# Adapter attention moved: scores and softmax into the front, its product into attention's steady part

## The reference

```python
q, k, v = split(h @ w_attn.T)                      # h: modulated layernorm of x
q, k = rope(q), rope(k)
y = softmax(causal(q @ k.T / sqrt(32))) @ v
_, ak, av = split(adapter_wte @ w_attn.T)          # 10 adapter tokens, no rope
s = q @ ak.T / sqrt(1024)                          # per head: 2048 x 10
y = y + gating[0] * softmax(s) @ av
x = x + ga * (y @ w_proj.T)                        # then a mixture of experts
```

## Time and profile before

| | us |
|---|---|
| median of 3 runs | 2719.55 (2714.84 to 2725.62) |
| the profiled execution, its own time | 2727.61 |
| its span, first to last instruction | 2725.7 |
| front | 0 to 679 |
| attention, head | 679 to 851 |
| attention, steady part | 851 to 1966 |
| its end, and the tail | 1966 to 2725.7 |
| busy PE / DVE / POOL / ACT over the span | 91% / 58% / 48% / 39% |

### The profile page before, as it was taken

The page is one execution under the profiler, slowest core; times in us unless marked ns, Lnnn a source line. Parts: engine busy times, 40 slices in busy tenths (PEclk is TensorE's granted clock), DMA queues, the critical chain, the costliest instruction groups (busy, mean ns, idle before and its releaser), DMA issues. The chain is left out here.

```text
span 2725.7 us, 39161 instructions
## 1 busy us (share of the span) xinstructions
PE 2491.5 (91%) x13391; PEld 1630.1 (60%) x13391; DVE 1593.0 (58%) x3130; ACT 1051.3 (39%) x1860; POOL 1313.7 (48%) x824
## 2 busy tenths in 40 slices
PE   6789999999578999999999999998889876999997
PEld 4667676777454444444444444443368765888885
DVE  5544554210256777777777777777236554777665
ACT  3420011111135655555555555555601111444443
POOL 4351442100365766676766676765724452332332
PEclk8899999999589999999999999998989887999998
DMA  7356556311953524252515151513266745888885
GB/s 265 109 155 201 160 165 183 100 39 51 223 202 103 113 55 111 56 115 54 116 49 120 42 131 40 133 34 79 77 203 216 168 113 183 305 299 294 302 287 178
DMA packets 224849, 397.18 MB, mean 146 GB/s; under 512 B 43756, under 2 KB 94380, under 8 KB 224564
## 3 DMA queue, kind: packets, MB, share of 16 engines
q1 hardware_dynamic: 199588, 319.56, 40.9%
q0 software_dynamic: 17152, 50.38, 5.3%
q10 hardware_dynamic: 7952, 25.21, 2.9%
HBM read 299.16 MB, written 103.76 MB: 148 GB/s over the span
## 5 line engine op out<-in xcount | busy, mean ns | idle before, releaser
L1397 POOL TENSOR_TENSOR t_two<-t_prob 128x1024 f32<-128x1024 f32 (+1 forms) x321 | 688.2, 2164 | 181.1 <-ACT t_prob L1207 107.7
L1207 ACT ACTIVATE t_prob<-t_scores_psum 128x512 f32<-128x512 f32 (+3 forms) x1280 | 611.1, 537 | 387.8 <-PE t_scores_psum L999 194.9
L1237 DVE TENSOR_REDUCE t_part<-t_seen_psum 128x1 f32<-128x512 f32 x768 | 480.8, 681 | 165.3 <-PE t_seen_psum L976 161.0
L976 PE MATMUL t_seen_psum<-t_k_stack,t_q_stack 96*128 96x512 f32 (+3 forms) x1283 | 517.1, 412 | 24.2 <-DVE t_part L1237 15.8
L999 PE MATMUL t_scores_psum<-t_q_stack,t_k_stack 97*128 97x512 f32 (+3 forms) x1280 | 506.1, 407 | 5.9 <-ACT t_prob L1207 4.4
L999 PEld LDWEIGHTS t_scores_psum<-t_q_stack,t_k_stack 97*128 97x128 f32 x1280 | 244.0, 191 | 310.0 <-ACT t_prob L1207 172.4
L1243 DVE CUSTOM_DVE_ANT_0 t_seen_psum<-t_seen_psum,t_causal 128x128 f32<-128x128 f32 (+3 forms) x515 | 250.0, 504 | 106.3 <-PE t_seen_psum L976 96.1
L1019 PE MATMUL t_y_acc_psum<-t_prob,t_v 128*32 128x512 f32 (+3 forms) x2560 | 304.9, 549 | 0.0
L976 PEld LDWEIGHTS t_seen_psum<-t_k_stack,t_q_stack 96*128 96x128 f32 x1283 | 253.2, 199 | 67.1 <-DVE t_part L1237 30.7
L1678 PE MATMUL acc_psum<-z_e_hi,z_x_hi 128*128 128x512 f32 x576 | 228.3, 396 | 0.0
L1680 PE MATMUL acc_psum<-z_e_hi,z_x_lo 128*128 128x512 f32 x576 | 225.2, 391 | 0.0
(11 more groups left out here) (240 smaller groups left out, 3804.1 us busy)
## 6 DMA issues: line engine op xcount, KB each, us to landing
z_raw<-in_expert_w SPq DMA_DIRECT2D x80, 512.0 KB, 5.3
z_spare<-in_expert_w SPq DMA_DIRECT2D x72, 512.0 KB
f_w_raw<-in_wmod SPq DMA_DIRECT2D x8, 2048.0 KB, 10.1
t_q_stack<-scratch_q_hi SPq DMA_DIRECT2D x64, 256.0 KB, 5.3
t_k_stack<-scratch_k_hi SPq DMA_DIRECT2D x64, 256.0 KB, 5.2
f_w_raw<-in_w_attn SPq DMA_DIRECT2D x24, 512.0 KB, 6.1
t_inverse<-scratch_inverse SPq DMA_DIRECT2D x132, 64.0 KB
t_y<-scratch_a_y SPq DMA_DIRECT2D x33, 256.0 KB
```

The lines of the kernel that those rows point to most:

```text
L976: nc.tensor.matmul(seen[:, n % BANKS, 0:width], q_stack[par][0:STACK, h, t0:t0 + P], k_stack[par][0:STACK, h, c * CH:c * CH + width], star ...
L1207: nc.scalar.activation(prob[:, step % RING, h, c0:CH], scores[:, score_bank(step, h), c0:CH], ACT.Exp, scale=1.0 / math.sqrt(D)).then_inc( ...
L1237: nc.vector.tensor_reduce(dst, seen[:, n % BANKS], AX.X, ALU.max).then_inc(seen_free, 1)
L1397: nc.gpsimd.tensor_tensor(two[:, pair % 2, heads, c0:CH], a, b, ALU.add).then_inc(two_ready, 1)
```

## The change

The adapter's scores and softmax move into the front's q units. Ask number m (m = 0 to 31, one per q unit) multiplies the rotated `y` of unit 32 + m with the adapter's k, inside the next unit, behind 21 of its 24 matmuls. DVE subtracts the maximum (`lower`), ACT takes the exponential (`exponent`), DVE sums and inverts (`invert`), POOL multiplies (`spread`), SP stores 80 KB of probabilities to `a_prob_d`. POOL's `low_y` of a q unit now also waits for its ask, since it overwrites `y`.

In attention the head keeps only the loads, the fills and the maxima. The adapter's v is scaled by the gating, written to DRAM and loaded again per group (`load_v`). The transposes and the product become two new kinds of entry in `order`, `ask` (6 steps behind a unit's end) and `give` (8 steps), each through one bank of the ring. An `ask` is four transposes of the loaded probabilities, which DVE copies to `a_turn` (`keep_turned`). A `give` is one float32 product of 512 columns; DVE's `divide` is moved behind it and its add reads the bank. The load of `a_y` goes. For the unit before the first there is nothing to compute, and four transposes of the identity keep the counts (`hold`).

```diff
@@ front
+                    if k == ASK_AT and asked(n) >= 1:
+                        ask(asked(n) - 1)
...
+            def ask(m):
+                pe.wait_ge(y_ready, n + 1)
...
+                for j in range(TPC):
+                    last = nc.tensor.matmul(turned[:, m % 2, j * HG * A:(j + 1) * HG * A], y[:, n % 2, j * P:(j + 1) * P],
+                                            ak[:, i * HG + s].rearrange("p (h a) -> p h a", a=D)[:, :, 0:A], start=True, stop=True)
+                last.then_inc(scored, 1)
...
             def low_y(n):
                 pool.wait_ge(y_hi_done, n + 1)
+                if asked(n) >= 0:
+                    pool.wait_ge(scored, asked(n) + 1)
@@ attention
-    ITEMS = sum(items_of(qc) for _, qc in UNITS) + W
+    ITEMS = sum(items_of(qc) for _, qc in UNITS) + 3 * W
...
-    Y_LAG, TOTAL_LAG, INV_LAG, DIVIDE_LAG, A_LAG, SPLIT_LAG, STORE_LAG = 2, 4, 5, 8, 6, 8, 9
+    Y_LAG, TOTAL_LAG, PROB_LAG, INV_LAG, ASK_LAG, GIVE_LAG, SPLIT_LAG, STORE_LAG = 2, 4, 3, 5, 6, 8, 8, 9
...
+        given = sorted(((last_step(wi) + lag) % STEPS, lag, what, wi - W * (last_step(wi) + lag >= STEPS))
+                       for wi in range(W) for lag, what in ((ASK_LAG, "ask"), (GIVE_LAG, "give")))
+        for step, _, what, wi in given[::-1]:
+            order.insert(until(AHEAD + PACE * step) + 1, (what, 0, wi, 0, 0, 0))
...
+            def give(n, into):
+                pe.wait_ge(a_turn_ready, n + 2)
+                pe.wait_ge(a_v_loaded, 16 * (n // NQ + 1))
+                nc.tensor.matmul(into, a_v[:, :], a_turn, start=True, stop=True).then_inc(seen_ready, 1)
...
+                elif what in ("ask", "give"):
+                    dve.wait_ge(seen_ready, i * ITEMS + real_of[i][n] + 1)
+                    (keep_turned if what == "ask" else divide)(i, qc, seen[:, n % BANKS])
+                    dve.sem_inc(seen_free, 1)
...
-            def divide(i, wi):
+            def divide(i, wi, at):
                 n = i * W + wi
                 dve.wait_ge(inverse_loaded, (n + 2) * (16 * HG))
                 dve.wait_ge(y_free, n + 2)
                 own = y_own[:, wi % 2]
-                nc.vector.tensor_tensor(own, own, inverse[:, :], ALU.mult).then_inc(norm_step, 1)
+                nc.vector.tensor_tensor(own, own, inverse, ALU.mult).then_inc(norm_step, 1)
                 dve.wait_ge(norm_step, n + 2)
-                dve.wait_ge(a_loaded, (n + 2) * 16)
-                nc.vector.tensor_tensor(y[:, :], y[:, :], own, ALU.add).then_inc(y_ready, 1)
+                dve.wait_ge(stored, (n + 3) * 32)
+                nc.vector.tensor_tensor(y[:, :], at, own, ALU.add).then_inc(y_ready, 1)
+                dve.wait_ge(y_ready, n + 3)
```

More of the change, by code:

```diff
@@ L511, in _ @@
                     split_w((half + 2) * HG - 1)
+            for m in range(QUERIES - 3, QUERIES):
+                spread(m)
             even_w(5 * HG, 4 * HG + 3)
@@ L1083, in _ @@
[L1083 to L1085 removed]
+            for n in range(HEAD):
+                if order[n][0] == "see" and order[n][3:] == (0, 0, 0):
+                    pe.wait_ge(first_loaded[order[n][2]], LOADS - 16)
+                advance(0, n)
             for c in range(NQ):
```

407 lines of the change are left out of this document (189 added, 218 removed).

## The result

| | before | after |
|---|---|---|
| device time, us (median; range) | 2722.3 (2714.8 to 2725.6, 4 runs) | 2750.4 (2743.2 to 2753.6, 4 runs) |
| profiled execution, us | 2727.6 | 2743.2 |
| end of the front's products, from the span's start | 678.2 | 706.8 |
| first steady score | 851.2 | 782.3 |
| first steady score to the last step | 1115.2 | 1200.7 |

The ratio of the times is 1.0103, 95% interval 1.0073 to 1.0134: the changed kernel is 1.0% slower. The forecast was 2742 (2700 to 2780), slower with a chance of 0.63. Between the two profiled executions the difference is +15.6 us, where the sum of the steps was +22.5; between the medians it is +28.1. Each ratio compares fast runs alone; one run of the twelfth experiment, 3401.6 us at a mean granted clock of 0.65, was slow and is left out of its ratio.

A forecast was written before the change was run, and what follows sets the result against it. TensorE was taken to bound the front and steady part, a long loop between engines the head. Terms -104 +2.5 +24 +41 +23 +12 -14 +37 +1 gave +22.5 us: 2750 on the profiled 2727.6, 2742 on the median (2700 to 2780).

The forecast's parts named there:

- The head, -104 and +2.5: Attention's head keeps only maxima, first steady score near 747: -104 us; steady part then begins at a lower clock: +2.5.
- The front, +24: Front's q units: added matmuls 27 us, waits for y +3, less 4 and 2 where PE already waited: +24 us.
- the claim that asks find y ready but for a few: Front: asks wait for y only where GpSimd's splitting of weights makes DVE slow, +3 us in sum.
- The steady part, +99: Attention's steady part: PE's own work +41, stalls +23 and +12, what goes -14, the clock +37 us.
- PE's own work: Steady part: 32 asks of 0.44 us and 31 gives of 0.86 us on PE, 41 us.
- The worked example of step 31: Steady part, a long give: PE idles 1.6 us for the give's bank; the step grows from 3.78 to 5.85 us.
- 29 of 1.0 to 1.5 us each: Sign in the steady part: about 29 PE idle rows on the maxima's matmul, ending with the divide's add.
- What went: Steady part: add no longer waits for the adapter's output, about 12 us; 2 us hidden where DVE bounds: -14 us.
- The clock, +37: Steady part: 19 clock falls after PE's stalls for DVE, 1.95 us each, +37 us.
- the threshold read from thirteen stalls: Old steady part: a clock fall followed seven of nine stalls of 0.97 us or more, none of four of 0.4-0.9.
- The end, +1: After the steady part: one ask and one give remain, only PE's own 0.44 and 0.86 us count, +1 us.
- Rival 3: Steady part: the ring hides the DVE work, only PE's own work is added; -56 us, 2663 us; chance 0.1.

The follow-up runs named there:

- the twelfth experiment: The sixth experiment's kernel with the front's asks behind the last three matmuls of their unit instead of ahead of them: 2682.3 us, ratio 0.9852.
- The sixth experiment: Experiment 5's kernel with the adapter's five small loads issued behind the first quarter's loads and constants, and two casts on ACT instead of DVE: 2684.4 us, ratio 0.9821.
- experiment 5: Changed kernel with gives and asks last in their steps and the next group's adapter values loaded early: 2696.2 us, ratio 0.9866.
- experiment 2: Changed kernel with each give as the last entry of its step instead of second: 2693.7 us, ratio 0.9879.
- experiment 7: Changed kernel with the give's multiply by the inverse sums replaced by a copy of one column, so output is unscaled: 2757.6 us in one run.
- experiment 8: Changed kernel with a second DVE operation behind the give's multiply, to hold the bank 0.7 us longer: 2792.3 us in one run.
- experiment 9: Experiment 1's kernel with GpSimd's sums cut from up to 512 columns to 128, so softmax sums are wrong: 2703.9 us in one run.
- experiment 10: Changed kernel with gives last in their steps and the second DVE operation of experiment 8: 2697.2 us in one run.
- experiment 1: Changed kernel with DVE's multiply by the inverse sums done before the wait for the give's product: 2751.5 us, ratio 1.0099.
- experiment 3: Changed kernel with the next group's adapter values loaded earlier, ahead of the stores of y: 2738.7 us, ratio 1.0057.
- experiment 11: Changed kernel with one of the four matmuls of each ask in the front: 2722.0 us in one run.

## Why the prediction was right, and where its sizes were off

**The head, -104 and +2.5: measured -97.6 from the head's first issue on.** From the first maximum to the first steady score it took 48.0 us, as reckoned (48.4). The error is in the start: the first masked maximum came 23.0 us behind the first issue, not 16. Two things were missing: five small loads in front of the first quarter, and casts that took 2.0 us each beside GpSimd's fills. The sixth experiment changed both at once and brought the whole head from 71.0 us to 64.4, where the forecast was 64.5; what each of them costs was not parted. The lower clock at the start of the steady part cost 0.3 us, not 2.5.

**The front, +24: measured +28.7.** An ask costs PE 0.93 us, not 0.85: 30 instead of 27. Waits for y were 10.8 us, not 3; the 10.3 us of waits for the modulation weights went altogether, more than the 4 taken. The step that failed is the claim that asks find y ready but for a few: it left out that DVE itself waits for GpSimd (80.5 us), which is the likely cause. This profile's front is also the shortest of eleven; their mean is 2.8 us longer.

**The steady part, +99: measured +85.5.** PE's own work was forecast as 41 us. An ask's 0.44 us holds (step 17 of experiment 5 grew by just that). A give's 0.86 was too low: its next matmul starts 1.05 us behind it, and in experiment 2, without a stall, a long give's step grew by 1.05; that is 6 us more for 31 gives, and the stalls are smaller by as much. That the bank's hold makes the stall is shown by experiments 7, 8, 9 and 10, in both directions.

The worked example of step 31 came out near its length, 5.75 us without a fall against 5.85, but partly by luck. It had PE ready for the last maximum at 2.27 us and the bank free at 3.85, 1.6 us of idle. In the trace PE was ready at 2.85 and the bank was free at 3.47, 0.61 us of idle: PE's work in front was longer, and DVE's multiply took 0.69 us in its new place, not the 1.09 of the old one. In the whole steady part there are 31 idle rows with 18.3 us behind DVE's signal, instead of 29 of 1.0 to 1.5 us each. By kind, at the forecast's prices: long gives 1.12 us beyond own work (1.25), of which 0.19 are PE's work, 0.73 the stall, and 0.20 what second place costs without a stall (experiment 9 against 2); steps 7 and 47 about 1.1 (0.75); steps 11 and 51 about 1.5 with 1.0 of it back in the next step (-0.2 in all); asks 5.4 in all (12). What went was 12.6 us beyond the moved stalls (12). Not in the sum: 8 us for the load of the next group's values, which the prediction does not mention; where it was waited for, it landed 4.1 to 4.6 us behind its issue.

**The clock, +37: measured some 19.6 behind the long gives and part of the 8 us at the loads.** The direction was right: without the stalls (experiments 2, 7, 9) no fall stands behind a long give. The step that failed is the threshold read from thirteen stalls of the old trace, and by it the stalls as they were measured, 0.61 us, would have brought no fall at all; the falls were forecast from stalls put at over 1 us. Idle of 0.61 us at a long give was followed by a fall in 45 of 70 cases (12, 10, 14 and 6 of 14 in the changed kernel twice and experiments 1 and 3; 3 of 14 in experiment 11). DVE's stalls of 0.87 to 0.98 us in steps 11 and 51 were followed by one in none of 15 cases in the first four of these profiles, but in 2 of 3 in experiment 11; stalls of 1.33 us in 9 of 14. A fall cost about 1.6 us there, not 1.95. Ahead of the last half of round 3 there were 14 falls where 19 had been counted, 12 behind long gives and 2 behind waits for the values. The count also left out two waits of PE for ACT in step 68 of round 3 of the old trace, which were followed by a fall of 6.8 us:

```profile
1930.24 0.50 PE L999 MATMUL t_scores_psum<-t_q_stack,t_k_stack 97*128 97x512 f32 x1 [0.54 <-ACT t_prob L1207]
1931.25 0.49 PE L999 MATMUL t_scores_psum<-t_q_stack,t_k_stack 97*128 97x512 f32 x1 [0.50 <-ACT t_prob L1207]
```

The Trainium skill (TensorE: Matmul & The Clock Gate, "A second HAM failure mode: psum-queue depth-cycling") describes such falls from short pauses between banks. The traces agree with it, and against its rule of long pauses ("HAM oscillation — how this bites in real kernels"), as the prediction had it. What besides the stall decides over a single fall stays open: no run here varied it alone.

**The end, +1: measured -0.9.** Rival 3, the ring that hides DVE's work, came true only when the give was moved (experiment 2). That profile is 28 us below the one before, not 56: the front took 10 us more than the sum had for it and the head 4, the steady part 30.8 us instead of 20 (gives cost 1.05 us and not 0.86, and asks stayed in second place with their stalls), and the part behind the last step 5, which lies within what it scatters by (757.8 to 769.1 us in the profiles other than experiment 7's).

**The sum.** That +22.5 us came out near the measured +15.6 is partly luck. The falls were put 17.4 us too high, the asks' stalls 6.6 and the clock at the start 2.2. Against them stand 8 us of loads that nobody had counted, 6.4 too few for the head, 4.7 for the front and some 4 for the gives.

## What to carry to other kernels

Work put into a ring of banks is paid by how long its bank is held and by what the producer has to do before it needs that bank again. Try such an entry where the longest stretch of other work follows it: here the place of one entry was worth 2% of the time, and turned a change that costs 1.0% into one that gains 1.2%, and 1.8% with the asks moved, the values loaded early and the head put in order as well. Before an operation of DVE is moved, look at what GpSimd does at the new place.

## What the runs showed of the hardware

- A DVE operation on two SBUF operands is held up while GpSimd adds in SBUF: 1.59 us instead of 0.69 (experiments 1 and 9), 1.50 on the mean of 32 in experiment 1. A cast of one SBUF operand beside GpSimd's fills took 2.04 us instead of 0.23, while masked maxima that read a PSUM bank kept their 0.28 to 0.73 us beside the same fills. The Trainium skill (GPSIMD Engine Reference, "Specifications") says that GpSimd's SBUF interfaces are shared with VectorE, in contention with instructions in a 2-port mode or with two SBUF inputs; the traces agree for the multiply, which has two. In which mode the cast ran no run shows. The 1.09 us of the multiply in the earlier trace rows fits: it ended 0.56 us behind GpSimd's sums in the kernel before:

```profile
1230.64 4.72 POOL L1397 TENSOR_TENSOR t_two<-t_prob 128x1024 f32<-128x1024 f32 x2 [1.43 <-PE t_total_psum L1032]
```

- Rows that read alike, with the same stall of PE, came with and without a fall of the clock within one execution (5.75 and 7.40 us), and a fall stood behind 3 to 14 of 14 such stalls from one execution to another.
- An fp32 product of 40 rows and 512 columns kept the next matmul off PE for 1.05 us at the full clock; four fp32 transposes took 0.44.
